# A four-layer attention stack on one core: throwaway products on TensorE in the waits of norms and in front of the second layer's scores

## The reference

```python
# layer 0: RMS norm, gated recurrence, cross attention over 77 keys, FFN
x_norm = _rms(x, norm1_scale)
...
x_res = x + h_seq + mem_out + v * 0.1
x0 = x_res + gelu(_rms(x_res, norm2_scale) @ Wf1 + bf1) @ Wf2 + bf2
# layer 1: the query is normed, attends to the normed context; a rank-4 MLP; self attention
norm_F_L = _layernorm(x0, norm2_w, norm2_b)
attended = softmax(norm_F_L @ norm_X.T * 256**-0.5) @ norm_X
...
# layer 2: cross attention with 16 heads, then a layer norm over x + attended
# layer 3: Mamba block with an RMS norm in front, then a layer norm and cross attention
h = _mamba2_block(x2, ...)
out = h + attention(_ln(h), encoder_out) @ Wo
```

## Time and profile before

| what | value |
|---|---|
| median of 3 runs | 1120.12 us (1118.92 to 1121.39) |
| the profiled execution's own time | 1122.69 us |
| its span, first to last instruction | 1120.9 us |
| mean granted TensorE clock | 0.890 |
| PE busy | 932.0 us (83%), 4604 matmuls |
| DVE busy | 576.6 us (51%) |
| ACT busy | 420.3 us (37%) |
| chain that ended last, by engine | PE 56%, DVE 24%, ACT 10%, issue 8% |

### The profile page before, as it was taken

One profiled execution on the slowest core, in us unless ns is written; L12 is line 12 of the kernel. 1 busy time (PEld: TensorE's weight loads), 2 busy tenths in 40 slices (PEclk: granted clock), 3 DMA queues, 4 the chain that ended last, 5 costly groups with the idle time before them and its releaser, 6 DMA issues.

```text
span 1120.9 us, 11512 instructions
## 1 busy us (share of the span) xinstructions
PE 932.0 (83%) x4604; PEld 445.5 (40%) x4604; DVE 576.6 (51%) x818; ACT 420.3 (37%) x526; POOL 47.9 (4%) x39
## 2 busy tenths in 40 slices
PE   4975789966989998969679998968978897886978
PEld 2532234434334433427223536223455445542332
DVE  3326999996210321063633336056759494953452
ACT  4343222233441244144154342636641275124434
POOL 0000000030000000000120000000011000200000
PEclk9887889976999898986799796989989898987999
DMA  8000000000000000020000000000000000000000
GB/s 348 1 0 0 0 1 0 0 0 1 1 1 0 1 0 1 0 105 1 0 1 1 1 1 1 1 1 6 9 1 1 0 1 1 1 1 0 1 37 37
DMA packets 3435, 15.78 MB, mean 14 GB/s; under 512 B 832, under 2 KB 1344, under 8 KB 2752
## 3 DMA queue, kind: packets, MB, share of 16 engines
q1 hardware_dynamic: 3248, 13.07, 3.0%
q0 software_dynamic: 144, 2.10, 0.5%
HBM read 12.67 MB, written 2.10 MB: 13 GB/s over the span
## 4 chain that ended last, share of the span: by engine, by line
PE 56%; DVE 24%; ACT 10%; issue 8%; DMA 1%; DVEq 0%; POOLq 0%; SPq 0%; POOL 0%; ACTq 0%
PE ps L366 55%; DVE AR L1470 3%; DVE AR L1471 3%; ACT AR L571 2%; DVE AR L1756 1%; DVE AR L460 1%; DVE AR L1473 1%; DVE VB L582 1%; DVE AR L1606 1%; DVE AR L1743 1%; ACT AR L439 1%; DVE AR L1747 1%; DMA CX<-in_ctxT 1%; DVE AR L1752 1%; DVE AR L454 1%
## 5 line engine op out<-in xcount | busy, mean ns | idle before, releaser
L366 PE MATMUL ps<-AR,WA 128*128 128x512 f32 (+3 forms) x808 | 364.7, 615 | 25.1 <-DVE AR L460 6.3
L366 PEld LDWEIGHTS ps<-AR,WA 128*128 128x128 f32 (+2 forms) x808 | 154.5, 196 | 229.7 <-issue 197.7
L366 PE MATMUL ps<-AR,CN 128*128 128x512 f32 (+3 forms) x352 | 145.7, 668 | 37.8 <-DVE AR L457 21.6
L366 PE MATMUL ps<-AR 128*64 128x128 f32 (+5 forms) x680 | 101.7, 421 | 12.2 <-DVE AR L1745 5.3
L366 PEld LDWEIGHTS ps<-AR,CN 128*128 128x128 f32 (+2 forms) x352 | 50.6, 183 | 102.9 <-issue 52.9
L590 DVE TENSOR_TENSOR AR<-ps,AR 128x512 f32<-128x512 f32 x24 | 16.6, 691 | 120.5 <-ACT AR L576 120.5
L366 PEld LDWEIGHTS ps<-AR 128*64 128x64 f32 (+4 forms) x680 | 52.5, 166 | 48.6 <-issue 17.3
L582 DVE TENSOR_REDUCE VB<-ps 128x16 f32<-128x1232 f32 x32 | 45.3, 1440 | 46.2 <-PE ps L366 46.2
L571 ACT ACTIVATE AR<-ps 77x2048 f32<-77x2048 f32 x24 | 44.2, 1870 | 63.8 <-PE ps L366 63.8
L1209 ACT ACTIVATE AR<-ps 128x512 f32<-128x512 f32 x48 | 28.7, 597 | 97.5 <-DVE AR L1473 49.9
L1547 DVE SCALAR_TENSOR_TENSOR X<-ps,VC,X 128x512 f32 x8 | 5.6, 746 | 106.7 <-PE ps L366 106.7
(11 more groups left out here) (258 smaller groups left out, 1086.5 us busy)
## 6 DMA issues: line engine op xcount, KB each, us to landing
WA<-in_m SPq DMA_DIRECT2D x1, 2856.0 KB, 10.2
WA<-in_m SPq DMA_DIRECT2D x1, 2560.0 KB, 15.5
X<-in_xT POOLq DMA_DIRECT2D x1, 2048.0 KB, 9.1
WA<-in_m SPq DMA_DIRECT2D x1, 2048.0 KB, 20.4
out<-X SPq DMA_DIRECT2D x4, 512.0 KB, 3.1
WB<-in_m SPq DMA_DIRECT2D x1, 1024.0 KB, 22.3
AR<-in_rows SPq DMA_DIRECT2D x1, 640.0 KB, 9.8
WA<-in_m SPq DMA_DIRECT2D x1, 512.0 KB, 16.1
```

What stands on the lines that cost most here:

```text
L366: return nc.tensor.matmul(out, lhsT, rhs, start=first, stop=last)
```

## The change

A function `spin(n)` issues n products of the identity matrix with a 128x128 matrix of ones (both constants in SBUF) into the first 128 columns of PSUM bank 7 (or of bank 6). Nobody reads the result, nothing waits for it and it waits for nothing. A table gives two numbers for each norm: how many products stand before the first wait of `norm_pe`, and how many between the mean's products and the first wait on the squares. `r2` gets 16 and 8, `l1` 0 and 10, `r3` 0 and 8, `l3` 24 and 10; `r1` and `x3` get none. 24 more stand between the norm `l1` and the scores of layer 1. Nothing else is changed.

```diff
+        SPINS = {"r1": (0, 0), "r2": (16, 8), "l1": (0, 10), "x3": (0, 0), "r3": (0, 8), "l3": (24, 10)}
+
+        def spin(n, to=7):
+
+            for _ in range(n):
+                mm(ps[:, to, 0:P], cn("ident"), cn("ones"))
+
         def norm_pe(pe, p, j, sq, mean, units=BS, at=bank, meanwhile=None):
+            spin(SPINS[p][0])
             if mean:
                 for b in units:
                     pe.wait_ge(*after("norm_sum", CENTRED[p] + n2(j, b)))
@@ -428,6 +436,7 @@
             if meanwhile:
                 meanwhile(0)
                 meanwhile(1)
+            spin(SPINS[p][1])
             for b in units:
                 pe.wait_ge(*after("norm_sqs", NORMS[p] + n2(j, b)))
@@ -865,6 +874,7 @@
             norm_pe(pe, "l1", 0, SQ1, True, UNITS, bank1)
+            spin(24, 6)
             for q in UNITS:
                 b, span = part_of(q)
                 pe.wait_ge(*after("f", DC * (q + 1)))
```

## The result

The changed kernel took a median of 1124.95 us (six runs, 1123.0 to 1127.5), the kernel before, on the same chip, 1120.36 us (six runs). The ratio is 1.0043, with a 95% interval of 1.0027 to 1.0059: slower by 0.4%, and 1, no change, lies outside the interval. Its profiled execution took 1126.41 us (span 1124.6), 3.72 more than the one before.

What follows compares the result with a forecast made beforehand. PE, busy 83% of the span, was taken as the bound, its clock falling after waits in norms. Terms -6.7 + 2.5 + 5.5 + 0 = +1.3 us on 1122.69 gave 1124.0, less 2.6: 1121.4 us, range 1115.5 to 1126.5.

Steps and rivals of the forecast that it cites:

- The scores: Layer 1's 64 score instructions run at full instead of half clock behind the throwaway products: 6.9 us less.
- The term for an earlier start: Layer 1's scores start at 503.4 instead of 504.22: 0.8 us gained, bounds 0 and 1.3.
- The 1.0 given back behind the scores: Behind layer 1's scores PE stands still, the clock falls and small products lose: +1.0 us, bounds 1.2 gained and 2.5 lost.
- r2: Throwaway products delay the real ones: +2.25 us each half, second half's FFN returns 2.0; sum +2.5, bounds +0.5 and +9.
- `l3`, first half: Throwaway products start at half clock and delay the mean: +3.6 us, 0.9 returned by the queries; +2.7, bounds +1.5 and +6.5.
- Second half: In l3, throwaway products at full clock make L454 4.65 us later; the queries behind return 1.8 us.
- The largest piece: The scores of layer 1 are the largest stretch at half clock: 13.94 us at 0.50 from end to end.
- 1 (the clock falls inside the scores): In layer 1's scores the clock falls again, the 6.9 us are lost: 1127.3 us, slower; chance 0.10.
- 2 (the first half of `l3` all at half clock): Throwaway products in front of l3 stay at half clock, 10.5 us instead of 7.3: +3.2, 1124.6 us; chance 0.12.
- 3 (more returned): Clock holds past the scores into the transposes; l3's first half and the FFN gain more: 1117.0 us, faster; chance 0.20.
- 4: Weight loads don't follow the clock, so layer 1's scores keep their pace: 1127.3 us, slower; chance 0.03.
- 5 (cheaper, or not delaying): Throwaway products are cheaper than their step or don't delay the real ones: 1114.4 us, faster; chance 0.05.

Runs made afterwards that it cites:

- only_l1: Kernel before with only the 10 throwaway products in norm l1 and the 24 ahead of layer 1's scores; 1114.77 us, ratio 0.9938.
- only_r2: Kernel before with only the 24 throwaway products of r2 in each half, none ahead of the scores; 1126.63 us, ratio 1.0041.
- only_l3: Kernel before with only the 24 and 10 throwaway products of l3 in each half; 1127.68 us, ratio 1.0064.
- fitted_x3: The fitted version with 10 more throwaway products between mean and squares of x3; 1115.35 us, ratio 0.9955.
- fitted_12: The fitted version with 12 instead of 24 throwaway products ahead of layer 1's scores; 1119.82 us, ratio 0.9987.
- placed: The fitted version with 28 throwaway products added once in layer 3, ahead of the wait for x4, outside the loop over halves; 1111.65 us, ratio 0.9905.
- the fitted version: Changed kernel with r2 8 instead of 24, l3 without its 24, r3 none; 1112.62 us, ratio 0.9922; run again 1109.62 us, ratio 0.9896.

## Why the prediction was right and where it was not

The time, 1124.95 us, lies in the range (1115.5 to 1126.5), 3.6 us above the forecast of 1121.4. But the likeliest case, no change, did not come; what came had a chance of 0.32. And that the time lies in the range is in part luck. In the trace the change cost 3.7 us where the sum had 1.3 (the remaining 1.1: the profiled execution lay 1.5 above the median and not 2.6). The terms for the touched places were short by 7.2 us together, 1.1 at `l1` and the scores, 3.8 at `r2` and 2.3 at `l3`; stretches that the change doesn't touch, for which the sum had no term, gave back 4.7.

- **The scores: right.** Forecast 6.9 us less, measured 6.67, at clock 1.00. The weight loads went along: the mean load of the scores lasts 192 ns where it lasted 332. The Trainium skill ("TensorE: Matmul & The Clock Gate", section "LDWEIGHTS (loading the stationary operand)") gives the time of a load as its columns over 1.2, without the clock; these loads do not agree with that. The term for an earlier start, -0.8, was too hopeful: the scores began as late, relative to what lies before them, as before (504.22 + 4.75 = 508.97, measured 509.00), since the 24 took 5.52 us and the squares' first product came 5.5 us later than before, 0.7 more than the rest: behind a pause of 2.32 us the clock fell under the mean's products (5.37 us for eight instructions; 3.67 before, behind the same pause). In `only_l1`, where it held there, the scores began 0.7 us earlier. The 1.0 given back behind the scores came as sized here; in `only_l1` nothing was given back by L1571, and 0.4 by L1606 (551.1).
- **`r2`: the step that failed.** The prediction put 48 x 0.11 = 5.3 us on the throwaway products, at a clock that holds. In the changed kernel the clock fell inside them, in both halves, and they took 7.22 us: +4.1 instead of +2.25 each. The -2.0 at the second half's FFN came. With +2.2 for the second half the term is +6.3, not +2.5. Where the clock did hold (`only_r2`), +2.5 twice shows that queueing was rightly reckoned; the clock was what I took as given. The upper bound of +9 covered it; the value taken lay too low.
- **`l3`, first half: right** (+3.1 against +2.7; the products took 7.95 us against 7.3). **Second half:** +4.65 forecast, +4.7 measured, but the 1.8 that the queries were to return did not come: PE stands still for 2.07 us in front of them, the clock falls, and six of their instructions take 4.54 us. That term had no reason: the pause stood in front of the queries before the change too (the earlier trace rows show its 2.07 us), and nothing in the change fills it. The windows, before and after:

```profile
1076.23:1081.00 4.77, 4.77 (x7) 2.02 (x8) 1.18 (x1) 0.69 (x1) 0.00 (x0) 0.64 0.00 0
1079.90:1084.60 4.70, 4.66 (x7) 2.03 (x8) 1.23 (x1) 0.69 (x1) 0.00 (x0) 0.64 0.00 0
```

- **`r3`: right,** 0.
- **Not in the sum:** -3.2 us at layer 2's scores, the largest of the stretches that gave back. It had a clock of 0.50 for 13.65 us before and for 3.4 us after:

```profile
616.70:630.35 13.65, 13.13 (x180) 10.97 (x184) 9.77 (x8) 0.00 (x0) 0.00 (x0) 0.50 0.00 1
622.70:626.10 3.40, 3.14 (x16) 1.83 (x20) 2.55 (x3) 0.00 (x0) 0.00 (x0) 0.50 0.00 0
```

`only_l3`, which is the same program as before up to there, shows 3.0 of it too, so it takes no throwaway product to come about: the clock falls at another moment in another execution.
- **The largest piece: wrong.** The prediction took the scores of layer 1 for the largest stretch at half clock. Layer 2's second half has a longer one, behind a pause of 4.90 us; the change doesn't touch it, it is as long after, and no run put throwaway products right in front of it (the 10 of `fitted_x3` stand ahead of that pause, and the 256 instructions behind it take 14.42 us with them as without). Before:

```profile
681.52:705.41 23.89, 21.28 (x288) 17.16 (x292) 14.86 (x15) 3.54 (x5) 0.00 (x0) 0.50 0.01 2
```

- **Rivals.** 1 (the clock falls inside the scores): no, 1.00 to the end; in `only_r2` and `fitted_12`, with a pause in front of the scores, it did fall inside them. 2 (the first half of `l3` all at half clock): no, 7.95 us and not 10.5. 3 (more returned): the added return came at layer 2 and not where I looked, and was outweighed. 4: no. 5 (cheaper, or not delaying): no; step 0.115 us, and the real products wait.

The failure has one form in both places: I counted on the clock where PE had just stood still for 1.9 or 2.1 us. The runs show that it can fall behind such a pause, 0.2 to 1.5 us into the work that follows, in `r2`'s throwaway products, in `l3`'s queries, in `fitted_12`'s scores, and that it need not: in `only_r2` it held in both halves. What decides between the two is not shown.

## What to carry to other kernels

Throwaway products are a tool with a price: what they take beyond the wait is lost, since the real product queues behind them, so size them to the wait as it was and not to what the clock would like. Here the same idea gave 1.0043 with 24 in `r2` and `l3`, and 0.9896 to 0.9922 with 8 in `r2` and without the 24 of `l3` and the 8 of `r3`. They pay in front of long work that would otherwise run at half clock from end to end (13.94 us of scores), and here only when they reached up to its start: with a pause of 1.90 us left, the gain was gone.

## What was not expected of the hardware

- The clock fell 1.5 us into dense throwaway work at `r2` (0.97, then 0.56, then 1.00), after a pause of 1.88 us in front of it. Behind the same pause it fell in both halves of one execution and held in both of another (7.22 and 5.60 us for the same 48 instructions).
- The scores are paced by their weight loads: with 77 moving columns they go at 0.114 us an instruction, the throwaway products with 128 at 0.115, both with 128 columns loaded. In no trace here did they raise the clock by themselves (13.94 us at 0.50), but behind dense work they kept it (7.27 us at 1.00). With a pause in front they could begin at 1.00 and lose it 1 or 2 us later (12.97 us in `fitted_12`, 12.13 in `only_r2`). So the same instructions took 7.27 to 13.94 us by what PE did before them.
- When the clock falls varies from one execution to the next even where the program is the same: 3 us at layer 2's scores. Between L1606 and L1636 of layer 1, `only_r2`, `placed` and `fitted_12` are 3.5 us slower than the others, with a clock of 0.50 for 13.6 us there; up to layer 3 `placed` is the same program as the fitted version, whose two traces don't have it. Differences of that size in single profiled executions say nothing of a change as a whole; the medians of several runs do, as far as they differ by more than the 3 us between the two groups of the fitted version.
